# Four instruction streams around a mixer's slots: ScalarE evacuates first, and attention's lead-in starts one slot sooner

## The reference, cut to what matters

```python
h = _layernorm(x) * (1 + ca) + sa
x = x + ga * mixer(h)                  # in_proj, causal conv of 4 taps, silu, scan over 512 steps, gated rms norm, out_proj
h = _layernorm(x) * (1 + cb) + sb
x = x + gb * experts0(h)               # an expert counts only if it drew at most 640 of the tokens
h = _layernorm(x) * (1 + ca1) + sa1
x = x + ga1 * (softmax((h Wq + bq)(h Wk + bk)^T / 8) (h Wv + bv) Wo + bo)
h = _layernorm(x) * (1 + cb1) + sb1
x = x + gb1 * layernorm(h + top2_experts(h)) * gamma + beta
```

## Time and profile before

| | |
|---|---|
| median of 3 runs (lowest, highest) | 610.76 us (607.73, 611.75) |
| the profiled execution, and its span | 607.35 us, 605.5 us |
| TensorE (PE) busy in the span | 529.0 us, 87% |
| VectorE (DVE) | 448.2 us, 74% |
| ScalarE (ACT) | 337.1 us, 56% |
| GpSimd (POOL) | 286.6 us, 47% |

### The profile page before, as it was taken

How to read it: one execution, slowest core, us unless ns; L and a number is a source line. 1 busy time by engine, 2 the same in 40 slices (tenths; PEclk the granted TensorE clock), 3 DMA queues, 4 the chain that set the end, 5 groups by cost and what they waited for, 6 DMA issues and landing times.

```text
span 605.5 us, 13809 instructions
## 1 busy us (share of the span) xinstructions
PE 529.0 (87%) x3457; PEld 443.0 (73%) x3457; DVE 448.2 (74%) x1657; ACT 337.1 (56%) x917; POOL 286.6 (47%) x348
## 2 busy tenths in 40 slices
PE   4789999999999999796999999852999999999592
PEld 3568878787878787673677777741999999999341
DVE  2758888888888787874689999984666666666177
ACT  4776757575757574434456665520566556565134
POOL 2235352525252424321026666674566666666243
PEclk9799999999999999988899999975999999999697
DMA  9499999996000000000641111112222222222473
GB/s 271 108 270 182 172 177 169 168 174 141 2 19 2 17 2 18 17 3 18 183 150 42 42 37 36 42 51 59 59 73 69 68 71 70 65 75 61 136 195 105
DMA packets 76395, 54.79 MB, mean 90 GB/s; under 512 B 10524, under 2 KB 69408, under 8 KB 76184
## 3 DMA queue, kind: packets, MB, share of 16 engines
q1 hardware_dynamic: 70352, 43.39, 36.2%
q0 software_dynamic: 4320, 8.99, 4.4%
q10 hardware_dynamic: 1640, 1.45, 0.7%
HBM read 40.62 MB, written 31.58 MB: 119 GB/s over the span
## 4 chain that ended last, share of the span: by engine, by line
PE 63%; DVE 17%; issue 9%; ACT 6%; DMA 3%; POOL 2%; DVEq 0%; SPq 0%; ACTq 0%; POOLq 0%
PE bank L1859 11%; PE bank L1877 11%; PE bank L694 4%; PE bank L812 4%; PE bank L696 4%; PE bank L695 4%; PE bank L809 2%; PE bank L1729 2%; DVE nmx L1492 2%; PE bank L833 2%; PE bank L1745 2%; PE bank L741 2%; PE bank L804 2%; PE bank L752 2%; POOL queue L1284 1%
## 5 line engine op out<-in xcount | busy, mean ns | idle before, releaser
L1324 POOL DMA_INDIRECT results<-arena x71 | 76.0, 1070 | 54.3 <-ACT arena L1423 49.7
L1859 PE MATMUL bank<-front,arena 128*128 128x128 f32 x568 | 78.4, 282 | 1.1 <-issue 0.4
L1284 POOL DMA_INDIRECT queue<-arena,pos x64 | 63.0, 984 | 29.0 <-issue 13.8
L301 POOL TENSOR_TENSOR arena<-arena,half_neg 128x1 f32<-128x1 f32 x32 | 17.6, 549 | 124.4 <-ACT arena L451 124.4
L1877 PE MATMUL bank<-h_all,front 128*128 x568 | 75.2, 276 | 0.1
L1859 PEld LDWEIGHTS bank<-front,arena 128*128 128x128 f32 x568 | 70.6, 196 | 4.3 <-issue 2.9
L1877 PEld LDWEIGHTS bank<-h_all,front 128*128 128x128 f32 x568 | 69.1, 192 | 0.3 <-issue 0.3
L1642 DVE COPY arena<-arena 128x516 f32 x71 | 35.9, 505 | 42.4 <-PE bank L1859 35.6
L1417 ACT ACTIVATE front<-bank 128x128 f32<-128x128 f32 x71 | 19.7, 277 | 53.9 <-PE bank L1850 53.9
L694 PE MATMUL bank<-h_hi,wc_hi 128*128 128x512 f32 x96 | 44.5, 463 | 3.0 <-ACT arena L445 3.0
L1655 DVE TENSOR_SCALAR front<-bank,arena 128x128 f32<-128x128 f32 x142 | 42.8, 343 | 4.8 <-PE bank L1859 4.5
(11 more groups left out here) (283 smaller groups left out, 1450.7 us busy)
## 6 DMA issues: line engine op xcount, KB each, us to landing
queue<-in_pad_rows SPq DMA_DIRECT2D x8, 2178.0 KB, 34.4
arena<-queue SPq DMA_DIRECT2D x71, 66.0 KB, 1.8
rows<-mod_rows SPq DMA_DIRECT2D x8, 384.0 KB, 6.7
x_keep<-x SPq DMA_DIRECT2D x8, 256.0 KB, 2.8
arena<-in_w SPq DMA_DIRECT2D x1, 2048.0 KB, 9.0
h_all<-in_w SPq DMA_DIRECT2D x1, 2048.0 KB, 8.2
h_all<-results SPq DMA_DIRECT2D x8, 256.0 KB, 5.0
arena<-results SPq DMA_DIRECT2D x8, 256.0 KB, 5.0
```

The lines of the kernel that those rows point to most:

```text
L1284: pool.indirect_dma_start(k.queue, bass.IndirectOffsetOnAxis(ap=pos[:, s, i, c0 + j:c0 + j + 1], axis=0), row[:, s * NC + c0 + j, i, :], N ...
L1324: pool.indirect_dma_start(k.results, bass.IndirectOffsetOnAxis(ap=xg[:, c, D:D + 1].bitcast(I32), axis=0), yw[:, c, :], None).then_inc(S[f ...
L1859: mm = t_.matmul(bank[(2 if g < NG // 2 else 6) + p][:, g * P:g * P + P], wc[:, p, g * P:g * P + P], xt[:, p, :], start=True, stop=True)
```

## The change

On ScalarE, the turned bank is evacuated before c = 1's Exp and Silu and before attention's piece in the last slots; xn1 of sequences 3 to 7 comes right behind that evacuation at c = 3, ahead of the convolution's. On VectorE, nm1 of these sequences is made at the end of slot c = 2. Attention's slots from -6 on run one mixer slot sooner, and none is left in 35. The fused value weights take three slots in place of two: the product with Wo moves from -9 to -8, its copy from -8 to -7, and TensorE's wait for the copy from -8 to -5.

```diff
             def body(s, b, c, between=None):
@@ scalar_program @@
-                if front and c == 1:
-                    wait(act, "d_dax", f + 1)
...
-                    ac.activation(early[:], ones[:, 0:1], ACT.Silu)
-                if between:
-                    between()
                 if s in turned:
                     wait(act, "s_amm", turned[s] + 1)
...
                     ins.then_inc(S["s_aev"], 1)
+                if front and c == 1:
+                    wait(act, "d_dax", f + 1)
...
+                    ac.activation(early[:], ones[:, 0:1], ACT.Silu)
+                if 3 <= b + 3 < NB and c == 3:
+                    normed(b + 3)
+                if between:
+                    between()
                 if front and c == 0:
@@
-                g = b + 3
-                if g < NB and c == 3:
...
-                    ins.then_inc(S["l1_xn"], 1)
+                if b + 3 < min(3, NB) and c == 3:
+                    normed(b + 3)
@@ vector_program @@
-                if gl < NB and c == 3:
+                if gl < min(3, NB) and c == 3:
@@
                     v.tensor_tensor(h_lo[:, g % 2, 3:3 + SEQ], h_new[:], h_hi[:, g % 2, 3:3 + SEQ].bitcast(F32), ALU.subtract).then_inc(S["h_lo"], 1)
+                if 3 <= gl < NB and c == 2:
+                    wait(dve, "l1_rs", gl + 1)
+                    wait(dve, "l1_xn", gl)
+                    v.scalar_tensor_tensor(out=nm1[:], in0=mv1[:].rearrange("p c t -> p (c t)")[:, 0::2], scalar=-1.0, in1=rs1[:],
+                                           op0=ALU.mult, op1=ALU.mult).then_inc(S["l1_nm"], 1)
@@
-        beside = {28: (-9,), 29: (-8,), 30: (-7,), 31: (-6,), 32: (-5,), 33: (-4, -3), 34: (-2,), 35: (-1,)}
+        beside = {28: (-9,), 29: (-8,), 30: (-7, -6), 31: (-5,), 32: (-4,), 33: (-3, -2), 34: (-1,)}
@@ attention, vector @@
-                if m == BEGIN + 1:
+                if m == BEGIN + 2:
                     wait(dve, "pv_mm", 1)
                     v.tensor_copy(wvo[:], bank[1][:, 0:D])
@@ attention, tensor @@
                     t_.transpose(bank[0][:, P:2 * P], k.bv[:], ident[:]).then_inc(S["sc_mm"], 1)
+                if m == BEGIN + 1:
                     wait(pe, "sc_exp", 1)
                     t_.matmul(bank[1][:, 0:D], wvT[:], wo, start=True, stop=True)
                     t_.matmul(bank[1][:, D:2 * D], bvT[:], wo, start=True, stop=True).then_inc(S["pv_mm"], 1)
-                if m == BEGIN + 1:
+                if m == -5:
                     wait(pe, "f_cnt", 1)
```

More of the change, by code:

```diff
@@ L364, in flat_leaves, with normed @@
                 ac.activation(raw[:, 3:3 + SEQ], bank[n % 2][:], ACT.Copy).then_inc(S["f_ev"], 1)
+            def normed(g):
+                wait(act, "l1_nm", g + 1)
+                if g >= 2:
+                    wait(act, "res_1", g - 1)
+                    wait(act, "f_mm", ring["h", g - 2, 0] + 1)
+                for i in range(NC):
+                    ins = ac.activation(xn1[:, g % 2, i, :], x[:, g * NC + i, :], ACT.Identity, scale=rs1[:, i:i + 1], bias=nm1[:, i:i + 1])
+                ins.then_inc(S["l1_xn"], 1)
             def body(s, b, c, between=None):
@@ L424, in body @@
                     ins.then_inc(S["s_aev"], 1)
+                if front and c == 1:
+                    wait(act, "d_dax", f + 1)
+                    act.wait_ge(S["set_pool"], 1)
+                    if f >= 1:
+                        wait(act, "o_w", seventh["da", f - 1] + 1)
+                    ac.activation(da48[:].rearrange("p (i w) -> p i w", i=3)[:, 0::2, :], dax[:].rearrange("p (o w) -> p o w", o=1).broadcast_to([P, 2, NC * NH]),
+                                  ACT.Exp).then_inc(S["d_da"], 1)
+                    ac.activation(early[:], ones[:, 0:1], ACT.Silu)
[3 more added lines that the diff above has]
+                    between()
                 if front and c == 0:
```

## The result

The kernel before took 611.25 us in the median of 4 runs (607.73 to 612.84), the changed kernel 587.74 us (586.77 to 588.53).

The account below looks back on a forecast made before the run. TensorE was taken to set the pace, busy 28.0 of 30 us, so time comes from its waits: 8.0 + 2.4 + 3.6 + 3.9 = 17.9 us, giving 589.4 from the profiled execution or 592.9 by the median; forecast 591, range 586 to 599.

Parts of the forecast that it names:

- c = 1, 8.0 us: Steady part: evacuating the turned bank before Exp and Silu removes TensorE's wait at L833 entirely, 6 x 1.34 us.
- rival (c): Steady part: L833's wait only moves to the convolution at c = 2; 604.8 to 607.8, no change; chance 0.08.
- c = 3, 2.4 us: Steady part: L459 moves into ScalarE's 4.00 us wait, so TensorE's wait at z goes in 5 sequences.
- the 1.0 of the upper bound: Steady part: nm1 held behind GpSimd's L311 costs VectorE at most 1.0 us, 5 times; nothing taken on the path.
- Rival (b): Steady part: nm1 is held and VectorE becomes the bound, 5 x 1.0 us come back; 594 to 598; chance 0.10.
- L649's 1.25 us: Steady part, VectorE: a four-column operation's length, taken as a sign that GpSimd can hold small operations such as nm1.
- Slots 28 to 32, 3.6 us: End of mixer: TensorE's waits of 1.24 and 1.80 go; VectorE, then the bound, loses its waits for TensorE.
- VectorE's three waits: Slots 28 to 32: VectorE's waits for TensorE of 1.13, 0.75 and 1.75 us go, the last being TensorE's low clock.
- Slots 33 to 35, 3.9 us: End of mixer: one attention piece gone, 4.8 less 0.9 us added work; the first of two 2.10 us waits goes.
- rival (a): Last slots are a ring; removing a piece may only lengthen the next wait; end gives 3 us, 594 to 597; chance 0.18.
- the upper bound of 10.0: End of mixer: at most 3.6 + 4.8 = 8.4 us, and another 1.6 if a low-clock stretch left in goes.
- rival (d): Steady part: late GpSimd power L296 holds xn1 and ScalarE's queue behind it, then TensorE; slower; chance 0.03.

Follow-up runs that it names:

- the other two kernels with the old end: Kernel before with the turned rows' evacuation ahead of Exp and Silu: 598.65 us; kernel before with the moves of xn1 and nm1 alone: 606.68 us.
- two other kernels: Changed kernel with fused weights over two slots: with the old table too, ratio 0.970 (3.4 us low clock); with the new table, 0.973 (8.5 us).
- the third group: Four measurements on another chip, kernel before at 617.4 us; the changed kernel was run again there unaltered: ratio 0.961, 594.72 us.

## Why the prediction was right, and where its sum was off

**c = 1, 8.0 us.** The mechanism held: the wait goes, and L703 waits for nothing in its place, so rival (c) is out. The size was low, since the move alone gave 9.6. The step that was off is reading the price of a wait from its idle time; start to start was the right measure.

**c = 3, 2.4 us.** It gave 2.9 alone and 2.7 on top of the other move. The same error, smaller: a wait of 0.44 to 0.6 us five times.

**nm1.** It was held in all 5 sequences for 0.9 us, close to the 1.0 of the upper bound, and that cost nothing on the path, as taken. The Trainium skill, "SBUF — State Buffer", section "SBUF: two separate sides", gave the hold; the trace agrees, with 1.06 us beside L311 and 0.16 us away from it. Rival (b) was right about the hold and wrong about its price: VectorE's spare waits, 3 us a sequence, covered both the hold and TensorE's faster pace. Freed of the hold, VectorE only waited longer. The sign that the prediction drew on, L649's 1.25 us, was a hold too, by L308, as shown above.

**Slots 28 to 32, 3.6 us.** All waits named there went (one of 0.70 us, at L842, is new), and from the turn of Wv to slot 33's L752 (L761) it is 24.3 us before and 20.6 after: 3.7 less, though the value projection now stands in it. The value is a mixture, since one of VectorE's three waits was TensorE's low clock, as the prediction says. Taken apart, the move of the fused weights is worth 1.8 us of TensorE's idle time (up to 2.2, by the other two kernels with the old end), and 1.7 us of clock in this profile stood behind its 1.80 us wait: 3.5 to 3.9. Without the move two other kernels had 3.4 and 8.5 us of low clock in the end, of which 1.7 and all the 8.5 stood behind these two waits.

**Slots 33 to 35, 3.9 us.** From L752 (L761) to attention's own first L1735 (L1744) it is 15.8 us before and 10.9 after: 4.9 less, of which some 1.7 is low clock. So the amount without the clock, some 3.2, was near, but the cause was wrong. I reckoned that "one such piece is gone from here", from 4.83 us between two waiting matmuls. With the piece put back there the end is no longer (43.0 against 43.4). What shortens these slots is that ScalarE serves L421 before attention's piece: 3.7 us by itself. The prediction named that order for the first of the two 2.10 us waits and gave it no price of its own. The table alone, with ScalarE's old order, would give 2.4, so it isn't void, but beside the order it adds nothing. Dividing a stretch by its pieces was the error. I now read the 4.83 us as one pass around a ring of TensorE, ScalarE and TensorE again, which the order shortens at each pass; no run shows the ring by itself. The rule of rival (a), that taking a piece out only lengthens another wait, describes the table; but the order took its wait out for good, and the 3 us of (a) weren't the result. The waits of 1.14 us (slot 32) and 1.52 us (slot 33) that the prediction left out gave 0.9 us between them.

**The clock.** The forecast left low clock in the last slots and put 1.6 us for it into the upper bound only. Three stretches went, 5.1 us in sum, at most 1.75 of which the forecast had counted, in VectorE's third wait. That is most of why 591 was 3.3 us too high. Without clock the steady part and the end gave 12.3 + 5.2 = 17.5 us, against a sum of 17.9. The agreement of the two is partly luck, as the steady part gave 1.9 more than forecast and the end less. The end as a whole, 10.3, came out above the upper bound of 10.0 that I had for it (8.4 + 1.6). That attention's first L1744 stands at 271.68, where "near 271" was forecast, is luck as well: 20.9 us of gain ahead of it less the 3.3 of the head. And that the clock stayed high in the end of this profile is not the program's doing alone, since the same program lost 1.7 us there in its second profile.

**Slower, rival (d).** The power L296 ended at 114.38, and xn1 (L372) waited for nm1, 2.2 us in all in 5 sequences, inside ScalarE's idle time: in the sequence shown L456 still waited 2.13 us for TensorE behind it. TensorE's waits for L456, the evacuation queued behind it, are 1.1 us in 6, where they were 1.4.

## To carry to other kernels

Price a wait from start to start of the two instructions around it, against the same pair where it runs undisturbed, and price the low clock behind it apart: in the end of this mixer half of a 10 us gain was clock. When several edits could each remove one wait, try every one alone: here the table of slots looked like the cause when I read the streams, and a change of order on the engine that releases the wait did the work. To free an engine that is held for 1 us is worth nothing while it has waits of its own to spend: here 4.5 us freed gave no time. Where the low clock overlaps a wait, take the engine's idle time and not the length less the low clock.

## What the runs showed of the hardware

- The granted clock differs between executions of one program. In the head, which no kernel here changes, the low clock took 3.4 us in eight profiles, 5.1 in five and 6.8 in one, that of the changed kernel, and the heads with 3.4 us differ by up to 1.8 us among themselves (42.3 to 44.1). Behind the same 1.82 us wait it fell in one profile of the changed kernel and not in the other. So two profiles can differ by 3.4 us for no reason in the program, and a gain of that size must be read from several runs or from lengths less the clock. The Trainium skill, "TensorE: Matmul & The Clock Gate", section "What's actually happening", says that the watch over TensorE's activity runs free of the kernel and that the effect varies from run to run; the traces agree with the second, and no run here can show the first.
- Low clock doesn't end with the wait that it follows. With the fused weights over two slots the clock fell at the wait of 1.24 us and stayed at the lower level through a wait of 1.71 for some 17 us, though TensorE was busy 17.1 of 20 us; with the old table the same two waits (1.24 and 1.80) cost 1.7 us of clock in place of 8.5.
- A 128x4 product on VectorE lasts 0.16 us alone and 1.06 us beside GpSimd's 128x512 one that started 0.5 us earlier; it ended 0.02 us after it. A 128x4 TENSOR_SCALAR with one tensor read (L649) was held as well: 1.25 us in the four sequences in which GpSimd's L308 started 0.05 us ahead of it, 0.14 to 0.17 us in all eight of the changed kernel.
- The chips of the three groups differ by some 2% in the kernel before (609.3, 617.4, 622.6 us), while the ratio of the changed kernel to it was 0.962 when first measured and 0.961 in the third group. The profiles show where the chips differ: the steady part with both moves took 194.4 us on each of the three (194.45, 194.43 and 194.44), and the rest of the span behind the sixth L1744 took 302 to 303, 314 to 316 and 310 to 312 us.
